# Linear attention: the feature map moved from VectorE to ScalarE and GpSimd

## The reference

```python
qkv = x @ w_qkv.T + b_qkv
q, k, v = jnp.split(qkv, 3, axis=-1)          # then 16 heads of 8 columns
q_prime = jax.nn.elu(q) + 1.0
k_prime = jax.nn.elu(k) + 1.0
kv_cumsum = jnp.cumsum(jnp.einsum('bhtd,bhte->bhtde', k_prime, v), axis=2)
context = jnp.einsum('bhtd,bhtde->bhte', q_prime, kv_cumsum)
norm = jnp.einsum('bhtd,bhtd->bht', q_prime, jnp.cumsum(k_prime, axis=2))
out = context / (norm[..., None] + EPS)       # then out @ w_out.T + b_out
```

## Time and profile before

| | us |
|---|---|
| median of 3 runs | 1269.02 (1268.82 to 1271.01) |
| the profiled execution, its own time | 1272.34 |
| its span, first to last instruction | 1270.6 |
| linear attention within it | 1079.0 to 1168.8 |
| busy over the span: PE, VectorE, ScalarE, GpSimd | 1144.6, 933.6, 793.6, 840.0 |

### The profile page before, as it was taken

The page is one execution under the profiler, slowest core; times in us unless marked ns, Lnnn a source line. Parts: engine busy times, 40 slices in busy tenths (PEclk is TensorE's granted clock), DMA queues, the critical chain, the costliest instruction groups (busy, mean ns, idle before and its releaser), DMA issues. The chain is left out here.

```text
span 1270.6 us, 24455 instructions
## 1 busy us (share of the span) xinstructions
PE 1144.6 (90%) x8010; PEld 856.0 (67%) x8010; DVE 933.6 (73%) x2075; ACT 793.6 (62%) x2190; POOL 840.0 (66%) x809
## 2 busy tenths in 40 slices
PE   5899999999999999999999999999996485796395
PEld 4577677677767776776677677767774485454285
DVE  5877877787787779777878877787784455698464
ACT  5777776777767777677777777777762153333153
POOL 1587677857795766678577958666685444684454
PEclk9899999999999999999999999999999588898598
DMA  4100620090027005300900170020014122000123
GB/s 118 48 1 2 125 35 2 6 158 2 1 51 109 2 1 114 50 2 1 157 3 2 50 114 2 1 67 2 1 50 113 34 64 67 1 1 1 34 68 96
DMA packets 74987, 55.72 MB, mean 44 GB/s; under 512 B 8336, under 2 KB 63760, under 8 KB 74864
## 3 DMA queue, kind: packets, MB, share of 16 engines
q1 hardware_dynamic: 72368, 49.02, 19.4%
q0 software_dynamic: 2496, 5.13, 1.2%
HBM read 13.35 MB, written 24.01 MB: 29 GB/s over the span
## 5 line engine op out<-in xcount | busy, mean ns | idle before, releaser
L387 DVE TENSOR_REDUCE at_nmax<-at_ps 128x1 f32<-128x512 f32 (+3 forms) x640 | 373.8, 602 | 129.8 <-PE at_ps L555 126.7
L359 POOL TENSOR_SCALAR at_prob<-at_prob,at_scale 128x512 f32<-128x512 f32 (+3 forms) x312 | 427.9, 1387 | 1.8
L552 PE MATMUL at_ps<-at_k_st,at_q_parts 128*128 128x512 f32 (+3 forms) x640 | 284.8, 445 | 5.0 <-DMA at_q_parts<-at_q_parts 3.6
L469 ACT ACTIVATE at_prob<-at_ps,at_nmax 128x512 f32<-128x512 f32 (+3 forms) x416 | 259.1, 630 | 45.6 <-DVE at_nmax L387 43.5
L581 PE MATMUL at_ps<-at_probT,at_v 128*64 128x256 f32 (+1 forms) x2304 | 270.3, 374 | 1.6 <-DVE at_probT L410 1.4
L555 PE MATMUL at_ps<-at_k_st,at_q_parts 128*128 128x512 f32 (+3 forms) x640 | 254.2, 398 | 0.0
L482 ACT ACTIVATE at_probT<-at_ps 128x512 f32<-128x512 f32 (+1 forms) x288 | 164.9, 573 | 142.6 <-PE at_ps L566 131.2
L359 POOL TENSOR_SCALAR late<-late,at_scale 128x512 f32<-128x512 f32 (+1 forms) x168 | 225.7, 1358 | 1.6
L410 DVE COPY at_probT<-at_ps 128x512 f32<-128x512 f32 (+1 forms) x288 | 188.7, 655 | 51.4 <-PE at_ps L566 48.7
L566 PE MATMUL at_ps<-ident,at_prob 128*128 128x128 f32 x1440 | 219.6, 274 | 2.8 <-DVE at_probT L410 1.8
L581 PEld LDWEIGHTS at_ps<-at_probT,at_v 128*64 128x64 f32 x2304 | 152.5, 136 | 102.4 <-issue 41.1
(11 more groups left out here) (193 smaller groups left out, 1484.6 us busy)
## 6 DMA issues: line engine op xcount, KB each, us to landing
at_q_parts<-at_q_parts SPq DMA_DIRECT2D x64, 256.0 KB, 3.7
slots_in<-zeros SPq DMA_DIRECT2D x6, 1483.5 KB, 16.8
slots_in<-zeros SPq DMA_DIRECT2D x6, 1419.0 KB, 16.7
f_xs<-slots_in SPq DMA_DIRECT2D x46, 64.5 KB
late<-in_L_ffn_w_dram SPq DMA_DIRECT2D x1, 2048.0 KB, 9.2
late<-in_L_ffn_w_dram SPq DMA_DIRECT2D x4, 512.0 KB, 6.3
f_got<-slots_out SPq DMA_DIRECT2D x8, 256.0 KB, 3.7
out_dram<-x SPq DMA_DIRECT2D x4, 256.0 KB, 2.4
```

The costliest lines, as they stand in the source:

```text
L359: pool.tensor_scalar(cols, cols, scale[:, k, u, c:c + 1], None, ALU.mult).then_inc(s_fix["pool"], 1)
L387: dve.tensor_reduce(nmax[:, q % 2, 2 * i + h, c:c + 1], bank, AX.X, ALU.max, negate=True).then_inc(s_max, 1)
L469: act.activation(prob[ROW_HOME[j]][u][:, c * BANK:c * BANK + w], ring[use_of["score", p, j, i, h, c] % RING][:, 0:w], ACT.Exp, bias=nmax[: ...
L552: pe.matmul(bank[:, 0:w], q_hi[h][:, r * P:(r + 1) * P], keys, start=True, stop=False)
```

## The change

max(z, 0) is written by ScalarE, as `above` = relu(z), between `neg` and the copy of v. The sum `above` + `ex` is made by GpSimd, from two tiles in SBUF, into the same `qk`. VectorE's stage `features` is gone, and `features` enters GpSimd's table with offset 1, between `norm` and `outer`. `z` on PE now waits for `above` and v of the tile before in place of `qk` and v, since those are what reads the bank. `above` has two buffers. VectorE's product gets a wait for `qk`.

```diff
+        above = pair("above", [P, 2 * D])
...
 GpSimd:
+                    elif stage == "features":
+                        pool.wait_ge(s_ex, t + 1)
+                        if t >= U:
+                            pool.wait_ge(s_qTp, t - U + 1)
+                            pool.wait_ge(s_past, t - U + 1)
+                            pool.wait_ge(s_prod, t - U + 1)
+                        pool.tensor_tensor(qk[k][:, :], above[k][:, :], ex[k][:, :], ALU.add).then_inc(s_qk, 1)
...
-                in_turn({"norm": 0, "outer": 2, "state": 3, "bias": 4}, emit)
+                in_turn({"norm": 0, "features": 1, "outer": 2, "state": 3, "bias": 4}, emit)
...
 VectorE:
                         dve.wait_ge(s_sums, t + 1)
+                        dve.wait_ge(s_qk, t + 1)
...
-                    elif stage == "features":
-                        dve.wait_ge(s_ex, t + 1)
-                        if t >= U:
-                            dve.wait_ge(s_qTp, t - U + 1)
-                            dve.wait_ge(s_past, t - U + 1)
-                        dve.scalar_tensor_tensor(qk[k][:, :], z_ps[:, 0:2 * D], 0.0, ex[k][:, :], ALU.max, ALU.add).then_inc(s_qk, 1)
...
-                in_turn({"heads": 3, "features": 1, "y": 5, "sums": 2}, emit)
+                in_turn({"heads": 3, "y": 5, "sums": 2}, emit)
...
 ScalarE:
                         act.activation(neg[k][:, :], z_ps[:, 0:2 * D], ACT.Relu, scale=-1.0).then_inc(s_neg, 1)
+                        act.activation(above[k][:, :], z_ps[:, 0:2 * D], ACT.Relu).then_inc(s_above, 1)
...
 TensorE, before z:
-                            pe.wait_ge(s_qk, t)
+                            pe.wait_ge(s_above, t)
                             pe.wait_ge(s_v, t)
```

More of the change, by code:

```diff
@@ L1100, in linear_attention @@
         den, o, oT = sb("den", [P, HL]), pair("o", [P, HL, DL]), pair("oT", [P, P])
-        s_one, s_xb, s_den = sem("s_one"), sem("s_xb"), sem("s_den")
+        s_one, s_xb, s_den, s_above = sem("s_one"), sem("s_xb"), sem("s_den"), sem("s_above")
         s_stat, s_aggr, s_std, s_rstd = sem("s_stat"), sem("s_aggr"), sem("s_std"), sem("s_rstd")
```

## The result

The changed kernel takes **1343.07 us** (median of 4 runs, 1340.91 to 1344.49), against 1270.01 for the kernel before in the same comparison (1268.82 to 1272.94): a ratio of **1.0566, interval 1.0548 to 1.0583**, 73 us slower. The forecast was 1345, with a range of 1320 to 1364. The profiled execution took 1344.11 us with a span of 1342.4, both 71.8 more than before.

What follows compares the result with a forecast made beforehand. PE's own chain was taken to bound each 4.58 us round of the linear attention stage. A new chain through GpSimd's queue (53.0) and PE's slower clock (23.3) add 76.3 us: 1345 against the median, range 1320 to 1364.

Steps and rivals of the forecast that it cites:

- The queue: On GpSimd, `outer` queues behind the wait of `features` for the next tile's `ex`, closing a chain through each round.
- The steps of the chain: One round from `z` through ScalarE, `features`, `outer`, `sums` and `oT` to the next `z`: 8.19 us against 4.58.
- The price of the addition: GpSimd's addition of 256 columns was put at 0.67 us, bounds 0.43 and 0.91.
- The line's other end: The addition was priced by a line through the bias addition (128 columns, 0.456 us) and `outer` (1152, 2.173).
- the cheaper column: GpSimd's price per column taken from the trace rows, 1.68 ns, against 2.2 from the Trainium skill's page.
- The clock: PE's 3.3 us gap before `sums` drops its clock from 2.4 to 1.2 GHz in most rounds: 23.3 us more.
- 15 `sums` times 1.55: The clock's cost: each `sums` on PE at the lower level, 3.76 in place of 2.21, 23.3 us in all.
- +1.6: Change forecast from sums(14) to the end of the last addition to x, in us.
- The collision: VectorE's `o` may meet GpSimd's `features`; up to 4.5 us if GpSimd waits, put at zero.
- (1): Rival: PE's clock holds at the full level, rounds of 8.19, 53.0 us more, 1322; chance 0.13.
- (2): Rival: PE's clock stays down for the whole stage, rounds of 10.86, 94 us more, 1363; chance 0.30.
- (3): Rival: the round stays pipelined with PE as the bound, time no longer than before, some 1268.5; chance 0.05.

Runs made afterwards that it cites:

- e1: The changed kernel with `outer` ahead of `features` in GpSimd's table, all work kept: 1276.90 us, ratio 1.0046 to the kernel before.
- e3: The kernel before with one wait added: GpSimd's `outer` also waits for the next tile's `ex`; no work added or moved: 1317.32 us, ratio 1.0372.
- e4: The changed kernel with eight extra products, results unused, on PE ahead of the wait for `outer`: 1323.08 us, ratio 1.0404 to the kernel before.
- e6: The changed kernel with `features` last in GpSimd's table, behind `outer`, `state` and `bias`: 1287.51 us, ratio 1.0136 to the kernel before.
- e5: The changed kernel with GpSimd's addition made twice in each round, one after the other: 1363.77 us, ratio 1.0734 to the kernel before.
- e9: e6 without VectorE's `den` addition, so EPS is left out and the reciprocal reads the sum directly: 1269.09 us, ratio 0.9988 to the kernel before.

## Why the prediction was right

**The queue.** Right, and shown from two sides: order alone brings back 67 of 73 us (e1), and the wait alone, without any work, costs 46 (e3), of which 8 are longer `sums`.

**The steps of the chain.** `z` to the end of `ex` was put at 1.17 and took 1.17 after `z` (1154.37 to 1155.54); `features` to `outer` 0.67, measured 0.68 from start to start, with 0.72 as the length of one; `outer` to `sums` 0.06 (1158.47 to 1158.53). The sum, 8.19, is e4's round. The 52.2 us of e4 stand against 53.0. The price of the addition came out right on the chain, but partly by luck: 0.67 was a length, and the length is 0.72; the chain pays the 0.68 from start to start. The line's other end, `outer`, is a product with repeated inputs and not an addition. Between two additions, the 451 ns of 128 columns (bias) and the 722 ns of 256 (`features`), a column costs 2.1 ns, not 1.68; "the cheaper column" of the prediction is not that of an addition. The estimate from the Trainium skill's page "GPSIMD Engine Reference", section 3.1, was 0.74, and the length in the trace is nearer to that.

**The clock.** Right that it falls, and near in the sum (20.9 against 23.3), but by errors of opposite sign; that they nearly cancel is luck. The step that failed is the term "15 `sums` times 1.55". First, a `sums` wholly at the lower level takes 4.21, 2.00 more, not 1.55: the 3.76 of the earlier trace rows had the higher level back before its end. Second, it isn't paid in each round. Of the 15 `sums` that waited, three took 4.21, four 2.21 and eight between 2.98 and 3.90, mean 3.30: 16.3 us over 2.21. Third, it isn't paid in `sums` alone, as the forecast had it: from z(1) to z(15) the changed kernel took 134.43 and e4 113.41, 21.0 apart, and 4.7 of that is outside `sums`. Some 2.2 of it lie in the first three rounds (`z` 1.49 in z(2) and z(3) too), the rest in the other eleven: in the one from 1183.03, where the level was still down behind `sums`, the stretch from its end to the next `z` took 1.39 in place of 0.95. sums(14) ran at the full level, where I had counted it at the lower one, and so did the output projections after it (0.46 behind a gap of 3.13, in place of 0.76 behind 3.06 in the earlier trace rows). With sums(15), which came 3.96 after sums(14) in place of 4.21, that is why the table has -0.9 where I had +1.6.

**The collision.** Putting it at zero was right, and the reason holds: VectorE had time to spare. But it was larger and elsewhere than I thought. `o` met not `features` but `outer`, and took 868 ns in the mean instead of 312; `den`, which I hadn't considered, took 413 instead of 178. GpSimd, which was first in the rows read, lost next to nothing (`outer` 2197 against 2173). The rule of the Trainium skill's page "SBUF — State Buffer", section "Who interferes with whom", that the second of the two is held for the whole of the first, is what the rows show for `o`. `den` has one SBUF input and a constant, so the rule for two inputs doesn't cover it; that it is held too is shown by its rows alone (2.08 in e6, up to the end of `outer`). In e6 such a hold decides the time, since there the held instruction lies on the ring.

**The rivals.** (1) with the clock at the full level was put at 1322: that is e4's kernel, at 1323, once the gap is filled. (2), the clock down throughout, was 10.86 a round; the changed kernel isn't there, and e5, with a wider gap, comes near it in its `sums`, though its `z` is at 0.87 in most rounds. (3), a pipelined round, is reached by the order of e6 once the lock is gone (e9, without EPS), with 1269.09 where the forecast for it was 1268.5. It wasn't a matter of `ex` being there in time, as I had put it, but of `outer` standing in front.

**The range.** 1343 lies inside 1320 to 1364, close to the forecast: the chain was off by 0.8 (53.0 against 52.2), the clock by 2.4.

## What to carry to other kernels

An instruction moved onto an in-order queue brings its wait with it, and the price is paid by what stands behind it: before costing the instruction, list what is queued there with its inputs ready, and who waits for that (here a wait without work cost 46 us, and the 0.7 us of work behind the ready one cost 6 in one place, 17 in another, and nothing in a third kernel, which leaves EPS out). A chain that leaves TensorE a gap can be paid a second time in its clock, so a gap is best costed with the rows of products at both levels. And where a pipeline's time depends on the phase of two engines, a tiny instruction of the one that is held while the other works can hold the phase in a worse place; look for a short operation that ends exactly when a long one of the other engine does.

## What the runs showed of the hardware

**VectorE beside GpSimd.** Held until GpSimd's instruction ended: `o` (two SBUF tiles), 0.29 to 1.92 beside `outer`; `den` (16 columns and a constant), 0.17 to 2.08 in e6 and 1.99 in e3. Not held: the reciprocal (0.25 beside `features` in e9), the product that has one input in PSUM (1.36 beside `outer`, in e9 as in the earlier trace rows). `den` beside GpSimd's `norm` took 0.17 in the kernel before (1118.77, `norm` from 1118.41). That last one isn't explained: `norm` reads and writes SBUF as `outer` does. The other way round, GpSimd's bias addition took 0.55 where it began 0.05 behind `o` (e1, 1117.97), against 0.45 in the mean of the changed kernel.

**The price of a gap before `sums`.** The same products, six matrix instructions in 15 rounds, behind four gaps:

| kernel | PE idle before `sums` | mean `sums` | rounds at 2.21 |
|---|---|---|---|
| e4 | 1.55 in most rounds | 2.21 | 15 of 15 |
| e3 | 2.52 to 2.68 | 2.75 | 9 of 15 |
| changed kernel | 3.33 to 3.60 | 3.30 | 4 of 15 |
| e5 | 4.13 to 4.40 | 3.95 | none |

The kernels differ in the length of their rounds too, so of the four only e4 against the changed kernel shows the gap alone. Rounds with the same gap come out differently: 3.38 us idle was followed by 2.21 and by 3.32. From the fourth round on, the `sums` of the changed kernel took 2.21, 3.65, 3.32, 2.21, 3.90, 3.74, 3.43, 2.98, 2.21, 3.64, 3.31 and 2.21: they shrink from round to round and start again. Nor did a gap of that size always lower the level: near the end of the stage PE was idle for 3.06 us in the kernel before, where the clock of a half microsecond was down to 0.72, and for 3.13 us, up to 1235.93, in the changed kernel, where it stayed up:

```profile
1234.50:1235.00 0.50, 0.00 (x0) 0.00 (x0) 0.44 (x2) 0.00 (x0) 0.00 (x0) 1.00 0.00 0
```

What decides was not tested: the trace of before gave reason to expect the fall in most rounds, not to say in which. That e4's idle products bought 20 us is the other side of it: here work that nobody needs was cheaper than the gap.
